# A three-part decoder layer on one core: new order of the work in cross attention's 24 rounds, row maxima turned four heads at a time, fourteen batches in one pass of the loop

## The reference, cut to what matters

```python
q = _w8a8_linear(x, wq, bq)                  # 16 heads of 16 columns
k = cond @ wk.T + bk                         # cond: 1444 x 256 per batch
v = cond @ wv.T + bv
scores = einsum('bhnd,bhld->bhnl', q, k) * inv_sqrt_d + mask
attn = softmax(scores, axis=-1)
o = einsum('bhnl,bhld->bhnd', attn, v)
return _w8a8_linear(o, wo, bo)               # 8-bit rows times 8-bit weights
```

## Time and profile before

| | us |
|---|---|
| median of 3 runs (lowest, highest) | 3807.72 (3787.60, 3811.28) |
| the profiled execution | 3806.76 |
| its span, first to last instruction | 3804.8 |
| self attention, about 0 to 1003 | 1003 |
| cross attention, about 1003 to 3191 | 2188 |
| feed-forward, about 3191 to 3804.8 | 614 |

### The profile page before, as it was taken

The page is one execution under the profiler, slowest core; times in us unless marked ns, Lnnn a source line. Parts: engine busy times, 40 slices in busy tenths (PEclk is TensorE's granted clock), DMA queues, the critical chain, the costliest instruction groups (busy, mean ns, idle before and its releaser), DMA issues. The chain is left out here.

```text
span 3804.8 us, 90413 instructions
## 1 busy us (share of the span) xinstructions
PE 3463.3 (91%) x34308; PEld 2589.1 (68%) x34308; DVE 2185.0 (57%) x4117; ACT 1753.7 (46%) x3020; POOL 764.9 (20%) x785
## 2 busy tenths in 40 slices
PE   7999999998499999999999999999899996688987
PEld 6998999997256666656656666666666654576776
DVE  4444444444456666666666666566566663656654
ACT  3322322322255555555555555555455543444443
POOL 0000000001211111111111111111111110566665
PEclk9999999999799999999999999999999986799999
DMA  3000000000466565656646556665655631000000
GB/s 102 14 14 4 9 13 13 13 9 20 88 110 106 105 111 98 109 89 108 107 93 109 104 104 106 113 103 104 103 88 104 111 60 59 14 14 18 23 10 22
DMA packets 121988, 257.22 MB, mean 68 GB/s; under 512 B 18880, under 2 KB 99392, under 8 KB 118512
## 3 DMA queue, kind: packets, MB, share of 16 engines
q1 hardware_dynamic: 115968, 247.34, 35.5%
q10 hardware_dynamic: 5616, 4.23, 0.4%
HBM read 99.72 MB, written 9.83 MB: 29 GB/s over the span
## 5 line engine op out<-in xcount | busy, mean ns | idle before, releaser
L1349 DVE CUSTOM_DVE_ANT_0 ca_rowmax<-ca_rowmax,ca_msk 100x1444 f32<-100x1444 f32 x512 | 855.3, 1670 | 501.4 <-PE ca_rowmax L1160 498.5
L1088 ACT ACTIVATE ca_prob<-ca_unit 128x800 f32<-128x800 f32 x640 | 534.5, 835 | 427.4 <-PE ca_unit L1255 426.9
L1255 PEld LDWEIGHTS ca_unit<-ca_qs,ca_ks 99*128 99x128 bf16 (+1 forms) x6144 | 371.8, 100 | 330.4 <-issue 181.0
L1255 PE MATMUL ca_unit<-ca_qs,ca_ks 99*128 99x100 bf16 (+1 forms) x6144 | 478.3, 213 | 69.4 <-issue 37.6
L1160 PE MATMUL ca_rowmax<-ca_ks,ca_qs 96*100 96x512 bf16 (+1 forms) x1536 | 426.5, 387 | 26.3 <-DVE ca_top L1349 17.0
L1229 PE MATMUL ca_acc<-ca_prob,ca_vaug 128*17 128x100 f32 x12288 | 446.1, 259 | 4.5 <-issue 4.3
L1133 PE MATMUL ca_ring<-ca_wvT,ca_ctxT 128*128 128x256 f32 (+1 forms) x1536 | 427.0, 406 | 11.3 <-issue 7.5
L975 POOL TENSOR_TENSOR ca_key_part<-ca_key_rest,ca_key_part 128x512 bf16<-128x512 f32 (+1 forms) x192 | 210.1, 1101 | 1060.2 <-ACT ca_key_part L1036 1060.2
L1126 PE MATMUL ca_ring<-ca_ctxT,ca_wkT 128*128 128x512 f32 (+1 forms) x768 | 397.2, 608 | 4.7 <-PEq L57 3.6
L1133 PEld LDWEIGHTS ca_ring<-ca_wvT,ca_ctxT 128*128 128x128 f32 (+1 forms) x1536 | 272.1, 192 | 84.6 <-issue 39.1
L1229 PEld LDWEIGHTS ca_acc<-ca_prob,ca_vaug 128*17 128x17 f32 x12288 | 235.3, 98 | 91.9 <-issue 26.1
(11 more groups left out here) (286 smaller groups left out, 6221.8 us busy)
## 6 DMA issues: line engine op xcount, KB each, us to landing
ca_ks<-ca_key_part SPq DMA_DIRECT2D x768, 90.2 KB, 4.6
ca_ks<-ca_ks SPq DMA_DIRECT2D x64, 722.0 KB, 5.5
ca_ctx<-in_ctx SPq DMA_DIRECT2D x32, 1408.0 KB
ca_ks<-ca_ks SPq DMA_DIRECT2D x64, 361.0 KB, 8.6
ca_msk<-in_mask_BxSxS_ff SPq DMA_DIRECT2D x32, 564.1 KB
sa_w_stage<-in_L_attn_w_qkv SPq DMA_DIRECT2D x12, 512.0 KB, 5.4
sa_x_in<-in_x ACTq DMA_DIRECT2D x8, 400.0 KB
sa_x_res<-in_x SPq DMA_DIRECT2D x8, 400.0 KB
```

What stands on the lines that cost most here:

```text
L1088: act.activation(prob[:, r % 2], unit[:, :, 0:QUAD * N], ACT.Exp).then_inc(bu.freed[0], 1)
L1255: return pe.matmul(unit[0:rows(t), n, j * N:(j + 1) * N], ks[:, par, h, t * TL:t * TL + rows(t)], qs[:, par, h, :], start=(j == 0), stop=T ...
L1349: dve.tensor_tensor_reduce(rowmax[0:N, 0:S], rowmax[0:N, 0:S], msk[:, par, :], 1.0, -3.0e38, ALU.add, ALU.max, top[:, h:h + 1]).then_inc(b ...
```

## The change

Three things. `BODY` goes from 4 to 14, so that the loop has two passes of fourteen turns. `mr` is done for four heads at a time, in four tasks instead of two, each with its own top chain on DVE (after heads 3, 7, 11 and 15 instead of 7 and 15), its own four transposes and its own copy of 3x400 instead of 3x800. And the table `slots` has a new order throughout: the maxima of heads 4 to 15 are now computed in the turn that uses them, those of heads 0 to 3 in the turn before; more tasks stand in other rounds.

```diff
--- before.py
+++ after.py
@@ -690,7 +690,7 @@
     PAIRS = TILES // 2
     ROUNDS = NQ * PAIRS
     HALF = H // 2
-    BODY = 4
+    BODY = 14
     assert (B - 4) % BODY == 0 and BODY % 2 == 0 and TILES % 2 == 0 and ROUNDS % 2 == 0
 
     def pair_of(r):
@@ -701,30 +701,30 @@
 
 
     slots = {
...
-        17: (("km", 1, 0), ("ka", 1, 1), ("mx", 4), ("kp", 1, 1)),
...
-        20: (("mx", 6), ("kp", 2, 0)),
-        21: (("ka", 2, 1), ("mx", 7), ("km", 2, 0)),
...
-        23: (("mr", 0), ("km", 2, 1)),
+        0: (("mx", 4), ("va", 0), ("vp", 0), ("va", 1), ("mx", 5)),
...
+        20: (("kp", 2, 0), ("mf",)),
+        21: (("mx", 3), ("km", 1, 0)),
+        22: (("ka", 2, 1),),
+        23: (("mr", 0), ("kp", 2, 1), ("km", 1, 1), ("km", 2, 0), ("km", 2, 1)),
     }
     timeline = [t for r in range(ROUNDS) for t in slots[r]]
     values = [t for t in timeline if t[0] == "vp"]
@@ -736,7 +736,9 @@
             return -1
         if task[0] in ("ct", "ka", "kp", "km"):
             return 2
-        return 0 if task == ("mr", 1) or (task[0] == "mx" and task[1] >= HALF) else 1
+        if task[0] in ("mx", "mr"):
+            return 1 if task in (("mx", 0), ("mx", 1), ("mx", 2), ("mx", 3), ("mr", 0)) else 0
+        return 1
 
 
     whole = {"ka": "kp", "va": "vp"}
@@ -793,7 +795,7 @@
         qsplit = sb("qsplit", [N, H, TERMS, DH], BF16)
         qs = sb("qs", [FULL, 2, H, N], BF16)
         top = sb("top", [N, H])
-        top_rest = sb("top_rest", [N, HALF])
+        top_rest = sb("top_rest", [N, QUAD])
         top_part = sb("top_part", [N, H, 3], BF16)
         mask_top = sb("mask_top", [N, 1])
         mask_flag = sb("mask_flag", [1, 2])
@@ -1048,11 +1050,11 @@
                                    ring[bank][0:STACK, :].bitcast(BF16)[:, 0:HC * N], ACT.Copy)\
                         .then_inc(bn.freed[bank], 1)
                 elif task[0] == "mr":
-                    h0 = task[1] * HALF
+                    h0 = task[1] * QUAD
                     bank = bn.bank(task)
                     bn.wait_full(act, task, b)
-                    act.activation(qs[STACK:FULL, par, h0:h0 + HALF, :].rearrange("p h n -> p (h n)"),
-                                   ring[bank][STACK:FULL, :].bitcast(BF16)[:, 0:HALF * N], ACT.Copy)\
+                    act.activation(qs[STACK:FULL, par, h0:h0 + QUAD, :].rearrange("p h n -> p (h n)"),
+                                   ring[bank][STACK:FULL, :].bitcast(BF16)[:, 0:QUAD * N], ACT.Copy)\
                         .then_inc(bn.freed[bank], 1)
                 elif task[0] == "vp":
                     bank = bn.bank(task)
@@ -1166,10 +1168,10 @@
                     bn.wait_empty(pe, task, b)
                 tile, tile_b = ring[bank], ring[bank][:].bitcast(BF16)
                 if kind == "mr":
-                    pe.wait_ge(top_done, 2 * b + task[1] + 1)
-                    for j in range(HALF):
+                    pe.wait_ge(top_done, NQ * b + task[1] + 1)
+                    for j in range(QUAD):
                         last = pe.transpose(tile_b[STACK:FULL, j * N:(j + 1) * N],
-                                            top_part[:, task[1] * HALF + j, :], ident_b[0:N, 0:N])
+                                            top_part[:, task[1] * QUAD + j, :], ident_b[0:N, 0:N])
                 elif kind == "eo":
                     ba.wait_out(pe, ("acc",), b)
                     for g in range(NQ):
@@ -1244,9 +1246,9 @@
                         bn.wait_out(pe, ("mf",), b)
                         pe.sem_inc(pe_passed, 1)
                         masked[par] = pe.value_load(mask_flag[:, par:par + 1].bitcast(I32))
-                    if g % 2 == 0 and tiles[0] == 0:
-
-                        bn.wait_out(pe, ("mr", g // 2), b)
+                    if tiles[0] == 0:
+
+                        bn.wait_out(pe, ("mr", g), b)
                     bu.wait_empty(pe, ("u", r), b)
 
                     def head(n, j):
@@ -1348,11 +1350,11 @@
                     dve.sem_inc(passed, 1)
                     dve.tensor_tensor_reduce(rowmax[0:N, 0:S], rowmax[0:N, 0:S], msk[:, par, :], 1.0, -3.0e38,
                                              ALU.add, ALU.max, top[:, h:h + 1]).then_inc(bm.freed[0], 1)
-                    if h % HALF == HALF - 1:
+                    if h % QUAD == QUAD - 1:
 
                         bm.wait_out(dve, task, b)
-                        hs = slice(h - HALF + 1, h + 1)
-                        chain = Chain(dve, top_step, 2 * b + h // HALF, 3)
+                        hs = slice(h - QUAD + 1, h + 1)
+                        chain = Chain(dve, top_step, NQ * b + h // QUAD, 3)
                         chain.link(dve.tensor_scalar(top_part[:, hs, 0], top[:, hs], -1.0, None, ALU.mult))
                         chain.link(dve.scalar_tensor_tensor(top_rest[:], top[:, hs], -1.0, top_part[:, hs, 0],
                                                             ALU.mult, ALU.subtract))
```

More of the change, by code:

```diff
@@ L703, in cross_attention @@
     slots = {
-        0: (("mx", 8), ("va", 0)),
-        1: (("vp", 0), ("mx", 9)),
-        2: (("eo",), ("va", 1)),
-        3: (("vp", 1), ("ct", 0, 0), ("mx", 10), ("ex",)),
-        4: (("ey",), ("va", 2)),
-        5: (("mx", 11), ("vp", 2), ("qq",), ("va", 3)),
-        6: (("vp", 3), ("mx", 12)),
-        7: (("qx",), ("ct", 0, 1)),
-        8: (("qp",), ("ct", 1, 0), ("mx", 13), ("ct", 1, 1)),
-        9: (("va", 4), ("mx", 14)),
-        10: (("vp", 4), ("qs", 0), ("mx", 15), ("va", 5), ("ma",), ("qs", 1), ("vp", 5)),
-        11: (("ez",), ("mr", 1), ("mx", 0), ("ka", 0, 0)),
-        12: (("kp", 0, 0),),
-        13: (("ka", 0, 1), ("mx", 1)),
-        14: (("kp", 0, 1),),
-        15: (("km", 0, 0), ("mx", 2), ("ka", 1, 0), ("km", 0, 1), ("kp", 1, 0)),
-        16: (("mx", 3), ("ct", 2, 0), ("mf",)),
-        17: (("km", 1, 0), ("ka", 1, 1), ("mx", 4), ("kp", 1, 1)),
-        18: (("ct", 2, 1), ("mx", 5)),
-        19: (("km", 1, 1), ("ka", 2, 0)),
-        20: (("mx", 6), ("kp", 2, 0)),
-        21: (("ka", 2, 1), ("mx", 7), ("km", 2, 0)),
-        22: (("kp", 2, 1),),
-        23: (("mr", 0), ("km", 2, 1)),
[24 rows of a table added]
     }
```

## The result

The changed kernel takes 3930.14 us (median of 4 runs, 3920.64 to 3940.16); the kernel before, run beside it, 3802.51 (3787.6 to 3811.28). The ratio is 1.032, 95% interval 1.029 to 1.035: **slower, by 3.2%**. Its profiled execution took 3920.6 us, with a span of 3918.8 against 3804.8.

What follows compares the result with a forecast made beforehand. PE was taken to set the time in cross attention. From 3806.8 us, -22 -30 -40 +3 +105 +75 = +91 gave 3898 us, 2.4% slower; own range 3850 to 3950, 8-in-10 range 3805 to 3975.

Steps and rivals of the forecast that it cites:

- Fourteen turns a pass: Loop's back edge: one stop instead of six, 5 x 4.46 us saved, -22 us.
- The wait for `mr 0`: Turn's start: PE's 1.0 us wait for ACT's copy of the maxima goes in 30 turns, -30 us.
- Waits A, B, C: Turn's end, PE stands 1.5 us at `ka (2,1)` (A), 0.65 at `mr 0` (B), 1.4 at `va 0` (C): +105 us.
- X: Start of round 21's units on PE, the zero from which the three waits near the turn's end are counted.
- The clock: PE's granted clock: 25 falls of 1.6 us go (-40 us); two new falls a turn come, 2.5 us a turn (+75).
- Extra switches: PE's extra switches for the split maxima, taken as 0.1 us a turn, +3 us.
- What else moves: Remaining effects: later placement priced at zero, closest maxima nothing, mid-turn stops left as they are, bounded by -40 and +80 us.
- Rival 1: The three waits come at the turn's end but the clock does not follow: turns of 65.6 us, 3823 us, chance 0.14.
- Rival 2: The three waits fall beside PE's path, only the wait for `mr 0` goes: 3718 us, faster, chance 0.10.
- Rivals 3 and 4: Mid-turn stops: 3, they go with the back edges, -40, 3858 us, chance 0.10; 4, every turn has one, +80, 3978, 0.08.
- Rival 5: SP's later first placement delays the next batch's key product: at most 0.7 us a turn, +20, 3918 us; chance within forecast's 0.58.

Runs made afterwards that it cites:

- body14: The kernel before with `BODY` 14 instead of 4 and nothing else: 3780.5 us, ratio 0.994.
- Quads: The kernel before, its order and four turns a pass kept, with `mr` for four heads at a time in rounds 18, 23, 7 and 11: 3827.4 us, ratio 1.008.
- km10: The changed kernel with only `km (1,0)` moved, from round 21 to round 18: 3860.3 us, ratio 1.016 to the kernel before.
- kmboth: The changed kernel with `km (1,0)` moved from round 21 to 18 and `km (1,1)` from 23 to 20: 3855.9 us, ratio 1.014 to the kernel before.
- kmmid: kmboth with the first key product's halves in rounds 11 and 12 and the three context transposes after it in 13, 13 and 14: 3868.1 us.
- kmlate: kmboth with the first key product's first half moved from round 10 to the end of 12, its second from 11 to 13: 3912.4 us.
- quads14c: quads14b with `mx 4` ahead of `mr 0` in round 17: 3749.7 us, ratio 0.986 to the kernel before.
- early0: The kernel before with `BODY` 14, groups of eight heads, `mx` 2, 3, 5, 6, 7 a step earlier and `mr 0` in round 22: 3821.7 us, ratio 1.003.
- quads14b: Quads with `BODY` 14, `mr 2` moved into round 6 and `mr 0` into round 17: 3782.2 us, ratio 0.995 to the kernel before.

## Why the prediction was right, point by point

The forecast was 3898, in the range and on the right side; 32 us more were measured in the medians, 23 in the profiled executions. The mechanism was right: the three waits came where and as long as it had them. Two terms were far off, with opposite signs, and that the sum still came near is partly luck: clock and switches were to make PE's busy time 38 us longer (+75 - 40 + 3), and it grew by 49 for another reason.

- **Fourteen turns a pass, -22: right.** -24 in body14; on the changed kernel 16 in the medians and 24 in the profiled spans, with the times alone not enough to decide.
- **The wait for `mr 0`, -30: right in idle time** (23.8 us gone). Quads shows it too: the wait leaves.
- **Waits A, B, C, +105: right, a little high.** From X (1133.76 in the turn shown) A ended at X + 3.94 where I had 4.0, B at X + 6.65 (6.7), C at X + 11.03 (11.0). PE reached `ka (2,1)` 0.17 us later than I counted, so A was 1.3 instead of 1.5. In all 93.6 us. km10 and kmboth show the cause: `km (1,0)` earlier removes A and B together, `km (1,1)` earlier removes C.
- **The clock, +75 - 40: wrong in size.** One failing sentence is "I expect two falls, behind A or B and behind C". In 29 turns 14 falls began behind C and five behind A or B, 19 where I had two a turn. The other is "After 1.0 us of idle it fell in 25 of 30 cases": the 25 of the earlier trace rows are waits, and I took them for falls. In the trace of before a fall began within 2.2 us behind 14 of the 24 waits of 1.0 us for `ca_qs` (turns 1 to 30), and behind the other ten none did, so some 22 us could go and not 40. In all the changed kernel has 31 falls with 133 us at a lower granted clock, the kernel before 27 with 140 us. At half speed a fall costs half its length, so the clock's part is -3 us and not +35.
- **Extra switches, +3: wrong, this is the other term.** PE's busy time grew by 49 us. The groups of instructions account for 16, a third: the lines of the two that grew most, of the kernel before and then of the changed one, stand below (11.6 and 9.4 us more; others shrank). I had taken 0.1 us a turn for the switches.

```profile
L1126 PE MATMUL ca_ring<-ca_ctxT,ca_wkT 128*128 128x512 f32 x720 | 372.1, 605 | 0.0
L1171 PE MATMUL ca_ring<-ca_ident_b,ca_top_part 100*3 100x100 bf16 x485 | 33.2, 214 | 2.2 <-DVE ca_top_part L1360 2.2
```

```profile
L1128 PE MATMUL ca_ring<-ca_ctxT,ca_wkT 128*128 128x420 f32 (+1 forms) x720 | 383.7, 622 | 38.9 <-DVE ca_key_rest L1327 38.9
L1173 PE MATMUL ca_ring<-ca_ident_b,ca_top_part 100*3 100x100 bf16 x484 | 42.6, 213 | 14.4 <-DVE ca_top_part L1362 14.4
```

  The rest, some 33 us, is between the groups: their records overlap less. Part of it is stops too short to be listed. Measured at the full clock from the start of one PE record to the start of the next, stops of 0.1 to 0.6 us beyond what the same pair of instructions usually takes grew by 12 us, most of it at `va`, at `ct` and at `mr 0`; what makes up the other 20 is not shown. The step that failed is "What else moves" and its zero: I looked for the large waits of the new order and counted everything else as unchanged.
- **What lies outside the thirty turns**, +16, I did not count. The first full turn starts 12.9 us later in after, 8.9 in kmboth, 7.9 in kmmid and 1.9 in kmlate. There PE waits 10.2 us at `ct` (L1195) in after, but ACT's single wait for the placement ahead of that turn is as long in before (9.9 us) as in after (9.8 us), so what makes the difference is not shown.
- **Rivals 1 and 2.** Rival 2 fell: all three waits are on PE's path. Rival 1 was no nearer on the clock: its net -40 is 37 us below the measured -3, the forecast's +35 is 38 above. Its 3823 also lacks the small costs.
- **Rivals 3 and 4, the mid-turn stops.** Both fell. Before, "issue" had 63.1 us in 21 stops of these turns, six of them back edges of 4.8 to 5.6 us: 32 us in the other 15. After, 36.7 us in some 22 stops, one a back edge of 3.8: 33 us. They neither went nor multiplied. The rule I weighed for rival 3 (the Trainium skill, Runtime: NRT & Kernel Launch, Instruction fetch mechanics: a branch back outside the window forces a fetch, going on to the next block is mostly hidden) agrees with the back edge. No experiment aimed at the mid-turn stops, but the DMA records of these traces tell what stands before them. One stop of the kernel before, and the DMA view from 1823.7 to 1825.4:

```profile
1826.82 1.14 PE L1133 MATMUL ca_ring<-ca_wvT,ca_ctxT 128*36 128x256 f32 x3 [2.56 <-issue]
```

```profile
q8 instruction: 1, 0.02, 5.4%
```

  A packet of 16 KB on the queue named "instruction" ends at 1825.3, and PE goes on 1.5 us later. The packet records of the traces show the same at every mid-turn "issue" stop of 0.9 us or more, 14 in before, 12 in after and 10 in body14: such a packet ended 1.3 to 2.0 us before PE went on. Of the waits of that length with another cause this holds for none of 24 in before and for one of 62 in after, and for some 8% of moments taken at random. So these stops are very likely fetches of instructions that come late. Before's stand in turns 0, 8 to 14 and 24 to 29, not once in each pass of four turns, which fits that a longer pass changed little. The queue moved some 220 such packets in the thirty turns, so most caused no stop, as "mostly hidden" has it; why these did is not shown.
- **Rival 5, the placement.** In after itself it took 4.7 us at `ct` (L1195), inside its bound of 20. It is the next wait in line, though: once A, B and C are gone it takes 36.9. My 5.6 us of room came from a kernel in which the key product started a round later; I never worked out what it would be once the waits were repaired, and so kmboth's expectation missed by 60 us.

That the order, and not the four heads, brings A, B and C is shown by quads14c, which has the four heads and none of the three. The slower PE work is another matter. Reckoned as above (half of the time busy at the lower clock taken off), PE's busy time is 1854 us in before, 1876 in quads14c and 1900 in after: of the 46 us some 20 are there with four heads in nearly the old order too, though early0, with groups of eight, has 1877 as well. So neither the split alone nor the order alone accounts for it, and which part of the new order makes the small stops is not shown.

## What to carry to other kernels

Before a read-out or a split is put later on an engine with time to spare, follow the double buffer behind it: a 0.6 us instruction put off by three rounds held a POOL step, a DVE read-out and a bank that PE wanted, 60 to 70 us in all. Of a new order list every tile's distance in its bank, not only the tiles that the change is about, and expect the wait behind the one you remove; the good version came from moving one task at a time, with the waits view between. And what a wait costs beyond its own length has to be counted in falls of the clock in the trace, not in waits: several waits close together may share one, and here not every wait had one.

## What the runs showed of the hardware

- A wait of 1.0 us at a turn's start was followed by a fall of the granted clock to 0.50 in 14 of 24 cases (before). Three waits of 1.3, 0.6 and 1.3 us within 8 us of each other had falls beside them 19 times in 29 turns, and not two or three times a turn (after). In quads14b waits of 1.0 us at `mr 0` in 30 turns were followed by a fall 49 to 53 us into the turn in eight only.
- PE stood 4.8 to 5.6 us at each of six back edges of the loop in before and 3.8 us at the one in after. At all 36 of the mid-turn "issue" stops of 0.9 us or more in before, after and body14 a 16 KB packet of the instruction queue had ended 1.3 to 2.0 us before PE went on.
- Twelve small copies (90 KB each) issued by one queue took 11.7 us to issue, and the last had landed 20 us after the first was issued (1287.46 to 1307.53 in kmboth), with that queue taking 66% of the DMA engines' time from 1290 to 1308.
